# A gathered-weights kernel's last slot gets its own branch, with an f32 mixing product and three column parts

## What is computed

```python
x = x + einsum('bct,bcd->bdt', x, L0_weights[tok])          # x is (32, 64, 1024)
x = x + einsum('bct,bcd->bdt', x, L1_weights[tok])          # 64x64 matrices, chosen by batch
x = x + einsum('bsi,oi->bso', x, W) + 0.5 * lora            # W 1024x1024, rank-32 addition by batch
x = x + einsum('bsi,boi->bso', x, L3_weight[ids])           # 1024x1024, one of 8 by batch
```

## Time and profile before

| | |
|---|---|
| median of 3 runs | 394.82 us (394.56 to 395.0) |
| the profiled execution | 394.66 us |
| its span in the trace | 392.9 us |
| PE busy | 380.2 us, 97% of the span |
| DVE, ACT, POOL busy | 268.3, 231.2 and 123.3 us |

### The profile page before, as it was taken

How to read it: one execution, slowest core, us unless ns; L and a number is a source line. 1 busy time by engine, 2 the same in 40 slices (tenths; PEclk the granted TensorE clock), 3 DMA queues, 4 the chain that set the end, 5 groups by cost and what they waited for, 6 DMA issues and landing times.

```text
span 392.9 us, 7604 instructions
## 1 busy us (share of the span) xinstructions
PE 380.2 (97%) x1736; PEld 316.4 (81%) x1736; DVE 268.3 (68%) x285; ACT 231.2 (59%) x307; POOL 123.3 (31%) x163
## 2 busy tenths in 40 slices
PE   8999999999999999999999999899999999999990
PEld 8888888888888888888888887688888888888860
DVE  4746967865855958547967439953699546899563
ACT  3798859387232775244483549554677357777361
POOL 0000340100003000024865427763258434576400
PEclk9999999999999999999999999999999999999996
DMA  7984902740348475406526224742276322762223
GB/s 225 396 313 158 375 3 79 261 180 19 107 173 288 182 277 166 180 21 214 175 93 221 58 55 123 260 133 55 56 235 211 97 57 56 270 219 54 56 58 88
DMA packets 24219, 61.37 MB, mean 156 GB/s; under 512 B 1938, under 2 KB 2066, under 8 KB 24146
## 3 DMA queue, kind: packets, MB, share of 16 engines
q1 hardware_dynamic: 23808, 60.30, 46.1%
q10 hardware_dynamic: 338, 0.24, 0.2%
HBM read 52.15 MB, written 8.39 MB: 154 GB/s over the span
## 4 chain that ended last, share of the span: by engine, by line
PE 96%; issue 1%; DVE 1%; ACT 0%; POOL 0%; ACTq 0%; DVEq 0%; POOLq 0%
PE ps L1400 44%; PE ps L1286 13%; PE ps L1287 13%; PE ps L1288 13%; PE ps L1427 4%; PE ps L1313 4%; PE ps L1325 2%; PE ps L1257 1%; PE ps L1265 1%; DVE stage L1236 0%; DVE stage L1177 0%; ACT stage L706 0%; DVE aT L1214 0%; PE ps L1446 0%; ACT stage L798 0%
## 5 line engine op out<-in xcount | busy, mean ns | idle before, releaser
L1400 PE MATMUL ps<-ring,aT 128*128 x784 | 180.8, 389 | 0.0
L1400 PEld LDWEIGHTS ps<-ring,aT 128*128 128x128 f32 x784 | 147.1, 188 | 30.8 <-issue 0.4
L1286 PE MATMUL ps<-ring 128*128 128x512 f32 x224 | 88.3, 394 | 0.0
L1287 PE MATMUL ps<-ring 128*128 128x512 f32 x224 | 88.0, 393 | 0.0
L1288 PE MATMUL ps<-ring 128*128 128x512 f32 x224 | 87.9, 392 | 0.0
L429 POOL TENSOR_TENSOR aT<-xT,aT 128x512 fp32r<-128x512 f32 (+1 forms) x36 | 56.3, 1585 | 51.3 <-ACT aT L685 45.2
L1149 DVE TENSOR_TENSOR ring<-raw,ring 128x1024 f32 (+1 forms) x40 | 63.8, 1655 | 5.1 <-ACT ring L671 5.0
L694 ACT ACTIVATE aT<-ps 64x1024 fp32r<-64x1024 f32 x32 | 32.7, 1021 | 48.1 <-PE ps L1400 47.6
L1177 DVE TENSOR_TENSOR stage<-ps,stage 64x1024 f32<-64x1024 f32 x30 | 36.7, 1222 | 26.3 <-ACT stage L706 25.7
L1166 DVE TENSOR_TENSOR aT<-ps,aT 64x1024 fp32r<-64x1024 f32 x32 | 39.1, 1222 | 22.6 <-ACT aT L694 21.9
L1288 PEld LDWEIGHTS ps<-ring 128*128 128x128 f32 x224 | 42.6, 190 | 9.0
(11 more groups left out here) (82 smaller groups left out, 314.5 us busy)
## 6 DMA issues: line engine op xcount, KB each, us to landing
raw<-w3t SPq DMA_DIRECT2D x40, 512.0 KB, 4.4
ring_f<-xt SPq DMA_DIRECT2D x8, 1024.0 KB, 7.7
raw<-xt SPq DMA_DIRECT2D x8, 1024.0 KB, 5.1
out<-stage SPq DMA_DIRECT2D x30, 256.0 KB, 3.0
ring_f<-wt SPq DMA_DIRECT2D x4, 1024.0 KB, 7.4
xT<-xt SPq DMA_DIRECT2D x3, 1024.0 KB, 9.5
xT<-wt SPq DMA_DIRECT2D x2, 1024.0 KB, 15.2
ring_f<-xt SPq DMA_DIRECT2D x4, 256.0 KB, 6.4
```

Source lines behind the costliest of these rows:

```text
L1286: pe.matmul(dst, hi_of(qw)[:, k, cs], hi_of(qx)[:, k, :], start=start and k == 0, stop=False, skip_group_check=True)
L1287: pe.matmul(dst, hi_of(qw)[:, k, cs], lo_of(qx)[:, k, :], start=False, stop=False, skip_group_check=True)
L1400: last = pe.matmul(acc(i)[:, n, :], x3_split(i, k, start, P), ring[:, bass.ds(off + (part * D + n * 512), 512)], start=(k == 0 and j == 0) ...
```

## The change

Five things are done.

1. **A branch of its own for the last slot**, on every engine. A function `rest(i)` asks "is there a slot after i?"; if so the ordinary `slot(i)` and `rest(i+1)` follow, and otherwise, in an `Else`, the last slot's own code. Since the `Else` of an outer level stands behind all inner levels, the own code of slot 16 stands behind the code of slots 16 to 18 and behind the own code of slots 19, 18 and 17. Slot 15 is now an ordinary slot.
2. **Mixing in f32**: POOL adds high and low part of the mixing matrices into one 128x128 f32 matrix `last_mix` (block-diagonal for a pair), ACT copies the last slot's rows as they are into `last_row`, and one f32 product takes the place of the split and two. DVE's `last_lo` and the addition afterwards fall away.
3. **Columns as 512, 256 and 256**, in three banks: 16 products of 512 columns, `mix(15)`, 16 of 256, the mixing of part 0, 12 of 256, the mixing of part 1, the last 4 of 256, six idle products (`BRIDGE`), the mixing of part 2. DVE copies out parts 0 and 1, ACT part 2; SP stores parts 0 and 1 and ACT part 2.
4. **Fewer stores and waits at the end**: for a single last slot 3 stores in place of 4, and SP waits for a slot's store two slots later, in `store`, so that only `stored15` and `end` are left.
5. **Front**: W's tile is loaded, rounded and split before x's.

POOL also clears `last_mix` once, before slot 0.

```diff
             for k in range(HALF):
                 one = slice(k, k + 1)
+                sp.dma_start(raw_of(w_slot(0))[:, one, :], w_block(1, 1)[:, one, :]).then_inc(s(f"w_in0_{k}"), 16)
                 sp.dma_start(raw_of(x_slot(0))[:, one, :], x_block(1, 0)[:, one, :]).then_inc(s(f"x_in0_{k}"), 16)
-                sp.dma_start(raw_of(w_slot(0))[:, one, :], w_block(1, 1)[:, one, :]).then_inc(s(f"w_in0_{k}"), 16)
...
             def store(i, word):
                 rows, single = batches(word), get(word, SINGLE)
+                if i >= 2:
+                    sp.wait_ge(s(f"stored{i - 2}"), 32)
                 sp.wait_ge(s("staged"), 2 * (i + 1))
...
+            def rest(i, word):
+                if i == SLOTS:
+                    store_last(i - 1, word)
+                    return
+                with sp.If(n_slots > i):
+                    rest(i + 1, step(i, word))
+                with sp.Else():
+                    store_last(i - 1, word)
...
+            def last(i, earlier, word):
+                rows_hi(i - 1)
+                act.wait_ge(s("mixed"), i)
+                last_rows(i, 0)
+                mixed_cols(i - 1, earlier)
+                last_rows(i, 1)
+                last_rows(i, 2)
...
+            def last_slot(i, earlier, mine):
+                def columns(passes):
+                    end_products(i, mine, passes, 0)
+                    mix(i - 1, earlier[2])
+                    end_products(i, mine, passes, 1)
+                    mix_last(i, 0)
+                    end_products(i, mine, passes, 2, (0, END_AT))
+                    mix_last(i, 1)
+                    end_products(i, mine, passes, 2, (END_AT, KT))
+                slot_ready(i)
+                with pe.If(mine[2] < 1):
+                    columns(PAIR)
+                with pe.Else():
+                    columns(ALONE)
+                warm(BRIDGE, acc(i - 1)[:, 1, 256:512])
+                mix_last(i, 2)
+
+            def rest(i, earlier, mine):
+                if i == SLOTS - 1:
+                    last_slot(i, earlier, mine)
+                    return
+                with pe.If(n_slots > i + 1):
+                    rest(i + 1, *slot(i, earlier, mine))
+                with pe.Else():
+                    last_slot(i, earlier, mine)
```

More of the change, by code:

```diff
@@ L242, in build, with out_part @@
     BEFORE3, WBASE = HALF, HALF * OPERANDS
-    def out_half(row, n, rows=slice(0, T)):
-        return out[bass.ds(row, 1), rows, 512 * n:512 * (n + 1)].rearrange("a t d -> (a t) d")
+    def out_part(row, part, rows=slice(0, T)):
+        return out[bass.ds(row, 1), rows, END_COLS[part]].rearrange("a t d -> (a t) d")
     with nc.Block() as block:
@@ L389, in _ @@
                 word = step(i, word)
[L390 to L405, removed]
+            def rest(i, word):
[6 more added lines that the diff above has]
+                    store_last(i - 1, word)
+            rest(SURE, word)
+            sp.wait_ge(s("end"), 48)
         @block.gpsimd
@@ L472, in step @@
             def step(i, earlier, word):
[L473 to L478, removed]
+                following = slot_word(pool, i + 1)
+                slot_lo(i + 1, following)
                 if i == 0:
@@ L489, in step, with rest @@
                 return word, following
+            def rest(i, earlier, word):
+                if i == SLOTS - 1:
+                    mixers_last(word)
+                    return
+                with pool.If(n_slots > i + 1):
+                    rest(i + 1, *step(i, earlier, word))
+                with pool.Else():
+                    mixers_last(word)
             earlier = None
-            for i in range(SURE):
+            for i in range(ENDS):
                 earlier, word = step(i, earlier, word)
[L494 to L497, removed]
+            rest(ENDS, earlier, word)
         @block.scalar
@@ L771, in last @@
[L771 to L780, removed]
-                with act.Else():
[L782 to L795, removed]
-                        act.activation(stage[own, i % 2, cols], end_ps(i, h, n)[other, :], ACT.Copy).then_inc(s("end_cols"), 1)
-                with act.Else():
-                    act.activation(stage[0:T, i % 2, cols], end_ps(i, 0, n)[T:P, :], ACT.Copy).then_inc(s("end_cols"), 1)
+            def last_rows(i, part):
+                act.wait_ge(s("end_left"), part + 1)
+                act.activation(last_row[:, END_COLS[part]], end_acc(i, part), ACT.Copy).then_inc(s("end_rows"), 1)
@@ L1217, in last @@
-            def last(i, word):
-                single = get(word, SINGLE)
-                last_sum(i, single, 0)
-                last_lo(i, 1)
-                last_sum(i, single, 1)
-            def last_sum(i, single, n):
-                cols = slice(512 * n, 512 * (n + 1))
-                with dve.If(single < 1):
-                    for h in range(2):
-                        own = slice(h * T, (h + 1) * T)
-                        dve.wait_ge(s("end_cols"), 2 * n + h + 1)
-                        dst = stage[own, i % 2, cols]
-                        dve.tensor_tensor(dst, end_ps(i, h, n)[own, :], dst, ALU.add).then_inc(s("end_staged"), 1)
+            def last(i, earlier):
+                rows_lo(i - 1)
+                mixed_sum(i - 1, earlier)
+                dve.wait_ge(s(f"stored{i - 2}"), 32)
+                for part in range(2):
+                    dve.wait_ge(s("end_mixed"), part + 1)
+                    dve.tensor_copy(stage[:, i % 2, END_COLS[part]], end_ps(i, part)).then_inc(s("end_out"), 1)
```

220 lines of the change are left out of this document (107 added, 113 removed).

## The result

| | before | after |
|---|---|---|
| median, us | 394.69 (393.79 to 395.0, 6 runs) | 400.86 (400.18 to 401.7, 6 runs) |
| profiled execution, span, us | 392.9 | 399.8 (its time 401.7) |
| ratio to before | | 1.0167 [1.0151, 1.0183] |

The change makes the kernel 1.7% slower, 1.6 us more than the 399.3 forecast and inside its range. The profiled execution of after is the longest of its six, 0.8 us over their median; about that much of what follows is its own.

What follows compares the result with a forecast made beforehand. PE, busy 97% of the span, was taken to bound the kernel. 392.9 - 2.0 (last slot) + 4.4 (PE's stalls) + 2.2 (clock) = 397.5, with 1.77 beside the span 399.3 us; range 393.9 to 401.7.

Steps and rivals of the forecast that it cites:

- The front: Start of the kernel, W's tile ahead of x's: costs and gives nothing, bounded at 0.7 us either way.
- The long branch on PE: L1491, PE's far jump from slot 15 to slot 16's code: reached at 369.8, stall of 4.0 us, low end 2.5.
- The second stall, L1480: PE's skip over the pair's code right after the far jump: another fetch of 3.1 us, bounds 0 and 4.0.
- F = 377.9: Start of slot 16's first product on PE: 377.9 with both stalls, 373.44 without, a loss of 4.4 us.
- The clock: PE's clock falls after 4.3 us idle before slot 16 and stays low about 4.4 us: costs 2.2 us.
- the clock holds: Rival at slot 16: two stalls on PE, but its clock stays up; end at 397.1; chance 0.22.
- SP's jump: SP's far jump, now ahead of the last stores and on the path: 2.5 us.
- The last slot: End of the kernel: the last slot's new order, undisturbed, ends at 390.85 in place of 392.89, worth 2.0 us.
- End = F + 17.4: From slot 16's first product to the end: 8.44 us to `staged`, then 9.0 through SP's last stores.
- The queue must empty first: Rival at PE's far jump: the fetch starts only at 373.6, once queued products are done; 402.1 us; chance 0.13.
- The queue covers the branch: Rival at slot 16: PE's far jump ends while queued products run, no stall; 392.6 us, 0.6% faster; chance 0.09.
- One stall only: Rival at slot 16: L1480 finds its code, so PE stalls once and its clock holds; 394.0 us; chance 0.13.

Runs made afterwards that it cites:

- SP straight: The kernel after with the number of slots fixed at 17 on SP alone, so without its questions and jump: 398.3 us, ratio 1.0093 to before.
- PE straight: The kernel after with the number of slots fixed at 17 on PE alone, so without its questions and jump: 393.32 us, ratio 0.9973 to before.
- the two turned ladders: The kernel after with last slot's code in line, further slots in the Else, on all engines: 393.73 us; the same with SP's wait behind its jump: 393.42 us.
- the kernel of the last slot in line: The kernel after, its slot question turned round on all engines: last slot's code stands next, further slots in the Else: 393.73 us, ratio 0.9975 to before.
- the straight kernel: The kernel after with the number of slots fixed at 17 on all engines, no slot questions or jumps on them: 391.12 us, ratio 0.9911 to before.
- the two straight kernels: After and before, each with 17 slots fixed on all engines: 391.12 us (ratio 0.9911 to before) and 392.8 us (0.996).

## Why the prediction was right, point by point

**The front: 0.** Right by measurement in both directions (1.0003, and 1.017 against 1.0167).

**The long branch on PE: 4.0 us, reached at 369.8.** Reached at 369.70, took 4.83. The price from L1489 was low, and it is the term of PE's sum that was mis-sized. The trace shows where the time went. Behind each of PE's slow branches the instruction queue (q8) starts a packet of 16 KB, behind this one two, and the branch is over 1.3 to 1.5 us after the last of them has ended. The packet behind L1489 started after 1.67 us and took 0.94; the later-ending one behind L1491 started after 1.05 us and took 2.45 in after, and 2.59, 2.74 and 3.01 in the three kernels where the branch took 5.10, 5.12 and 5.49. In windows of 1 us, 370.7 to 371.7 of after and 387.4 to 388.4 of before (packets, MB, and the packet's time as a share of 16 us):

```profile
q8 instruction: 1, 0.02, 15.3%
```

```profile
q8 instruction: 1, 0.02, 5.8%
```

So what made this branch dearer is a slower packet of the same size, and not the distance by itself, 2169 instructions against 912. What slowed the packet, slot 14's stores, the second packet or the other engines' own code at that time, no run separates.

**The second stall, L1480: 3.1 us.** 3.18 in after, 2.98 with SP straight, 3.28 with PE straight, 2.64 with all straight, and 2.98 in the kernel with the front undone. The price was right: from L1491's end the packet for L1480 started 1.05 us later and its branch was over after 3.54, for the 3.4 in all that the prediction took. Its reason was only half right: the stall doesn't need a far jump ahead of it, since with straight code ahead it takes 2.6 to 3.3 us too. Nor do the 233 instructions decide it: in the two turned ladders the same skip took 0.33. Where it was long, a packet of q8 starts 0.34 to 0.69 us behind the branch's start and the branch is over 1.3 us after its end; where it was short, none starts during it (the kernel of the last slot in line fetched at 364.84 and next at 370.73, the branch stood at 369.64; the straight kernel fetched at 359.19 and next at 371.25, the branch stood at 370.91). So in these seven records what decides is whether the piece had been fetched already. With the single's code in line it took 0.08.

**F = 377.9, undisturbed 373.44, loss 4.4.** Measured 378.51, and undisturbed 373.00, where slot 15's products end: loss 5.5. The steps: first stall +0.83, question 0.10 earlier, second +0.08, and 0.45 from the second branch's end to the first product where 0.6 was allowed.

**The clock: 2.2 us.** It fell, and cost 2.7 (6.29 - 3.63); that is read from the trace, no run had the long stall without the fall. It stayed low for 6.8 us, 377.15 to 383.97, and not 4.4. The 4.4 rested on products 0.443 us apart at the front of before, where the window 9.50 to 14.10 reads 1.00; that this spacing belongs to the low level is shown by after, whose products stand 0.43 apart from 8.86 to 11.84 in the window at 0.50. Behind the idle times of 5.51 and 5.55 us at slot 16 it was down, behind that of 3.02 us it wasn't; before, behind 3.3 us at the end, it was the earlier trace rows. The rival "the clock holds" had two stalls and the clock up; no kernel showed that, the clock held only where one of the two was gone.

**SP's jump: 2.5 us.** 3.4 from L418 to L379 (392.11 to 395.5), and the first store 3.94 after the question where the sum had 3.1. Taken away alone it gives 2.6 us. With it gone from both engines, the end goes by the landing of the same stores, issued at 385.6 and 386.6 in the straight kernel.

**The last slot: -2.0 us.** 1.7 to 1.9 by the two straight kernels. The column chain did have room: ACT's last store stands at 392.89, F + 14.4 where the chain's sum up to this issue, with the clock, gives F + 14.2, and 3.2 us ahead of SP's first.

**End = F + 17.4, with the clock F + 19.6.** Measured F + 21.3. From `mix(15)` to `staged` 5.28 where 4.81 was taken (ACT's first copy of f32 columns, L795, goes ahead of `mixed_cols`, 386.55 - 384.80 = 1.75 for 1.27), and 9.7 where 9.0 was from there to the end. Terms over the forecast: F 0.6, clock 0.5, `staged` 0.5, SP 0.7, together 2.3, which is 399.8 less 397.5. All of them have the same sign, and the stalls of PE and SP, 1.3 of the 2.3, come from one choice: a price from one record, taken at its value, with the low bound taken seriously and no high one given. The profiled execution stood at 401.7, the very edge of the range; that the median lies 1.6 us over the forecast and not 2.4 is this execution's own 0.8.

**Rivals.** *The queue must empty first* falls: L1491 began at 369.70 and was over at 374.53 while products ran to 373.00; by that rival its 3.15 us or more would have begun at 373.0 and F would be past 380. *The queue covers the branch* is half right: in the straight kernels it covers one stall of 2.6 or 3.3 us to 0.18 and 0.47 us, and in the turned ladders one of 2.9 to 0.41 and one of 3.25 to 0.80. What it doesn't cover is two in a row, 8.0 us with a lead of 3.3 (373.00 - 369.70), nor a single one of 5.49, which left 3.02. *One stall only*: above.

The Trainium skill, page "Runtime: NRT & Kernel Launch", section "Instruction fetch mechanics", says that a taken branch whose target is not in the current two pages forces a fetch. The trace agrees for PE: behind every branch of 2.6 us or more a packet of 16 KB starts, and in L1480's two records of 0.33 us none does. On which page a target lies no trace shows, so for the 233 instructions the rule itself is not tested. The 2048 instructions that the same section gives TensorE are not seen: 233, 438 and 912 cost 2.6 to 4.2 us where they stalled.

## What to carry to other kernels

Put the code that the usual input runs in line and let the rare case jump: a taken branch over a few hundred instructions can cost 2.6 to 5.5 us on PE and cost 2.5 to 3.4 us on SP, ACT and DVE, and what covers it is a queue of waiting work, here some 3.3 us of it. Count every such branch between one piece of work and the next on each engine, the one to the program's end among them, and let each be asked while something else is under way, ahead of a wait and not behind it. A stall of PE may cost half as much again through its clock (5.5 us of idle time, then 2.7 at the low level), so where it is cut the gain can be more than its length.

## What the runs showed that was not expected

- L1480, a skip of 233 instructions, stalls PE for 2.6 to 3.3 us in five kernels, two of them with straight code ahead of it on PE, and takes 0.33 us in two others; the branches inside the slots have records up to 0.34 us in after. The long ones are those during which PE's queue fetches a piece.
- The same branch in the same place took 4.83, 5.10, 5.12 and 5.49 us in four kernels that differ little, and the difference is that of one 16 KB packet (2.45 to 3.01 us).
- After 5.5 us of idle time the granted clock was at 0.50 for 6.8 us, though PE was busy from 378.51 on, 5.5 us of it; after 3.02 us of idle time it had not moved.
- Four questions in line on SP, five branches in the trace, took 0.72 us, 0.14 a branch, at a place where nothing covers them.
- In before, the ladder cost 1.6 us of 394.4, and no row of PE's busy time shows it.
